# A transformer layer over 1,024 sequences on one Trainium2 core: the turn of x, a store and a load change their places in the step

## The reference

```python
q, k, v = ((x @ w + b) split into 8 heads of 16 features)
attn = softmax(q @ k^T / 4)                # per head, 128 x 128
out  = concat(attn @ v) @ wo + bo
n    = layernorm(x + out, ln1_g, ln1_b)
ff   = relu(n @ w1 + b1) @ w2 + b2         # 128 -> 512 -> 128
y    = layernorm(n + ff, ln2_g, ln2_b)
```

## Time and profile before

| | |
|---|---|
| median of 3 runs | 4271.92 us (4266.54 to 4272.6) |
| the profiled execution's own time | 4273.66 us |
| its span in the trace | 4271.9 us |
| granted TensorE clock, mean | 0.997 |
| busy: PE, PEld | 4104.8 us (96%), 3538.0 us (83%) |
| busy: DVE, ACT, POOL | 3669.8 us (86%), 3434.5 us (80%), 3723.4 us (87%) |
| DMA engines, mean busy share | some 0.8 in nearly every slice |

### The profile page before, as it was taken

The page is one execution under the profiler, slowest core; times in us unless marked ns, Lnnn a source line. Parts: engine busy times, 40 slices in busy tenths (PEclk is TensorE's granted clock), DMA queues, the critical chain, the costliest instruction groups (busy, mean ns, idle before and its releaser), DMA issues.

```text
span 4271.9 us, 150528 instructions
## 1 busy us (share of the span) xinstructions
PE 4104.8 (96%) x49930; PEld 3538.0 (83%) x49930; DVE 3669.8 (86%) x9740; ACT 3434.5 (80%) x5890; POOL 3723.4 (87%) x3864
## 2 busy tenths in 40 slices
PE   5999999999999999999999999999999999999997
PEld 4888888888888888888888888888888888888886
DVE  5888888888888888888888888888888888888885
ACT  4888888888888888888878888888888888888886
POOL 4888888888888888988888888888888888888987
PEclk9999999999999999999999999999999999999999
DMA  7788887888888888888778888887878888888883
GB/s 147 178 177 185 175 185 175 186 179 183 180 180 183 178 182 174 184 176 183 177 178 180 183 176 183 176 185 176 187 177 184 180 179 180 180 180 179 186 178 84
DMA packets 1970442, 755.81 MB, mean 177 GB/s; under 512 B 1181312, under 2 KB 1969536, under 8 KB 1969664
## 3 DMA queue, kind: packets, MB, share of 16 engines
q1 hardware_dynamic: 1662480, 605.71, 66.8%
q10 hardware_dynamic: 307184, 140.40, 12.3%
HBM read 202.51 MB, written 134.22 MB: 79 GB/s over the span
## 4 chain that ended last, share of the span: by engine, by line
PE 42%; issue 20%; ACT 10%; DVE 9%; SPq 5%; ACTq 5%; POOL 5%; DMA 3%; DVEq 1%; POOLq 0%
PE bankB L693 10%; PE bankC L693 9%; PE oT_ps L734 6%; SPq L252 5%; PE s_ps L707 5%; PE sT_ps L721 4%; ACT h_sb L397 4%; DMA stack<-parts 3%; PE bankC L670 3%; DVE xT_sb L502 2%; ACT parts L385 2%; PE bankA L670 2%; ACTq L430 2%; ACT parts L379 2%; PE bankB L670 2%
## 5 line engine op out<-in xcount | busy, mean ns | idle before, releaser
L417 ACT ACTIVATE prob_sb<-sT_ps 128x1024 f32<-128x1024 f32 x1024 | 1050.6, 1026 | 415.8 <-PE sT_ps L721 342.4
L547 DVE TENSOR_REDUCE max_sb<-s_ps 128x8 f32<-128x1024 f32 x1024 | 1220.2, 1192 | 6.9 <-PE s_ps L707 5.9
L278 POOL TENSOR_TENSOR parts<-rest_sb,parts 128x512 bf16<-128x512 f32 x512 | 584.4, 1162 | 243.0 <-ACT parts L385 243.0
L707 PEld LDWEIGHTS s_ps<-stack 96*128 96x128 bf16 x8192 | 463.9, 98 | 296.1 <-issue 181.4
L707 PE MATMUL s_ps<-stack 96*128 96x128 bf16 x8192 | 639.5, 221 | 42.0 <-DMA stack<-parts 24.0
L448 ACT ACTIVATE n_sb<-z_sb,shift,rs 128x128 f32<-128x128 f32 x1024 | 422.2, 483 | 276.1 <-POOL shift L323 276.0
L721 PE MATMUL sT_ps<-stack 99*128 99x128 bf16 x8192 | 627.9, 219 | 2.9 <-ACT prob_sb L417 2.9
L693 PE MATMUL bankB<-w_sb,h_sb 128*128 128x128 f32 x4096 | 525.2, 281 | 77.2 <-ACT h_sb L397 75.8
L693 PEld LDWEIGHTS bankB<-w_sb,h_sb 128*128 128x128 f32 x4096 | 476.5, 191 | 120.5 <-ACT h_sb L397 118.7
L734 PE MATMUL oT_ps<-prob_sb,v_ones 128*32 128x128 f32 x16384 | 554.0, 276 | 4.6 <-ACT prob_sb L417 3.3
L734 PEld LDWEIGHTS oT_ps<-prob_sb,v_ones 128*32 128x32 f32 x16384 | 416.4, 109 | 127.9 <-issue 89.4
(11 more groups left out here) (75 smaller groups left out, 8469.8 us busy)
## 6 DMA issues: line engine op xcount, KB each, us to landing
stack<-parts SPq DMA_DIRECT2D x3072, 128.0 KB, 3.6
x_blocks<-in_x SPq DMA_DIRECT2D x1024, 64.0 KB, 2.4
n_mem<-n_sb SPq DMA_DIRECT2D x256, 256.0 KB, 3.2
n_blocks<-n_mem SPq DMA_DIRECT2D x1024, 64.0 KB, 2.2
out<-out_sb ACTq DMA_DIRECT2D x256, 256.0 KB, 3.3
x_sb<-in_x ACTq DMA_DIRECT2D x255, 256.0 KB, 4.4
stack<-max_parts ACTq DMA_DIRECT2D x768, 8.0 KB, 2.2
h_sb<-in_L_conv_w SPq DMA_DIRECT2D x1, 256.0 KB, 3.1
```

The costliest lines, as they stand in the source:

```text
L278: pool.tensor_tensor(parts[:, r % 2, 3 * c + LO], rest_sb[:, c], parts[:, r % 2, 3 * c + MID], ALU.subtract).then_inc(lo_split, 1)
L417: act.activation(prob_sb[:, s % 2], sT_ps[:], ACT.Exp, scale=float(D) ** -0.5).then_inc(exp_done, 1)
L547: dve.reduce_max(max_sb[:, (r - lag) % 2, :, s], s_ps[:].rearrange("p (h k) -> p h k", h=H), AX.X).then_inc(max_done, 1)
L707: ins = pe.matmul(s_ps[:, h * P:(h + 1) * P], stack[0:PROD, (r - lag) % 4, 0, h, tok], stack[0:PROD, (r - lag) % 4, 1, h, tok], start=True ...
```

## The change

On VectorE, `turn_x` moves from behind the maxima of slot 0 to the head of the step, ahead of `turn_out(0)`. On ScalarE, the cast of `xT_sb` moves ahead of slot 0's exponential, and the issue of x's load moves from there to between `n_sb`'s and `m_sb`'s four applications. The output's store leaves ScalarE: SP issues it one step later (lag 9 instead of 8), between the store of n and the loads of x in blocks, and SP's loop therefore runs to lag 9. No instruction is added or dropped in the steady step and no tile changes its size.

```diff
--- before.py
+++ after.py
@@ -236,6 +236,9 @@
                 if live(t, r, 5):
                     sp.wait_ge(n_done, upto(t, r, 5, plus=1))
                     sp.dma_start(n_mem[(r - 5) % 2].rearrange("(s k) m -> k s m", s=SEQS), n_sb[:]).then_inc(n_stored, DMA)
+                if live(t, r, 9):
+                    sp.wait_ge(out_ready, upto(t, r, 9, plus=1))
+                    sp.dma_start(out_g[t + (r - 9)], out_sb[:, (r - 9) % 2]).then_inc(out_stored[(r - 9) % 2], DMA)
                 if live(t, r, -1):
                     if (v := upto(t, r, 0)) is not None:
                         sp.wait_ge(x_turned, v)
@@ -252,7 +255,7 @@
                             sp.dma_start(stack[j:PROD:len(Q_PARTS), r % 4, c].rearrange("d h x -> d (h x)"),
                                          parts[:, r % 2, 3 * c + part]).then_inc(stack_loaded[r % 2], DMA)
 
-            iterate(sp, step, 0, LEAD, LAST, 5)
+            iterate(sp, step, 0, LEAD, LAST, 9)
             sp.wait_ge(out_stored[(G - 2) % 2], upto_dma(0, G - 2, 0))
             sp.wait_ge(out_stored[(G - 1) % 2], upto_dma(0, G - 1, 0))
 
@@ -418,16 +421,12 @@
 
             def step(t, r):
 
-                exponentials(t, r, 0)
                 if live(t, r, 0):
                     act.wait_ge(x_turned, upto(t, r, 0, plus=1))
                     if (v := upto(t, r, 0)) is not None:
                         act.wait_ge(k_done, v)
                     act.activation(xT_parts[:, HI], xT_sb[:], ACT.Copy).then_inc(xT_hi, 1)
-                if live(t, r, 0) and (r > 0 or not isinstance(t, int)):
-                    if (v := upto(t, r, 1)) is not None:
-                        act.wait_ge(xb_done, v)
-                    act.dma_start(x_sb[:, r % 2], x_g[t + r]).then_inc(x_loaded[r % 2], DMA)
+                exponentials(t, r, 0)
                 if live(t, r, 7):
                     relu(t, r, 7, 2)
                     relu(t, r, 7, 3)
@@ -448,6 +447,10 @@
                         ins = act.activation(n_sb[:, s], z_sb[:, s], ACT.Identity, bias=shift[:, 0, s:s + 1],
                                              scale=rs[:, 0, s:s + 1])
                     ins.then_inc(n_done, 1)
+                if live(t, r, 0) and (r > 0 or not isinstance(t, int)):
+                    if (v := upto(t, r, 1)) is not None:
+                        act.wait_ge(xb_done, v)
+                    act.dma_start(x_sb[:, r % 2], x_g[t + r]).then_inc(x_loaded[r % 2], DMA)
                 if live(t, r, 8):
                     apply2(t, r, 8)
 
@@ -477,9 +480,6 @@
                                    ACT.Copy).then_inc(v_copied, 1)
                 if live(t, r, 2):
                     max_row(t, r, LO)
-                if live(t, r, 8):
-                    act.wait_ge(out_ready, upto(t, r, 8, plus=1))
-                    act.dma_start(out_g[t + (r - 8)], out_sb[:, (r - 8) % 2]).then_inc(out_stored[(r - 8) % 2], DMA)
 
             act.wait_ge(qk_loaded, N_QK * DMA)
             act.wait_ge(v_ones_set, 1)
@@ -575,11 +575,11 @@
 
             def step(t, r):
 
+                if live(t, r, 0) and (r > 0 or not isinstance(t, int)):
+                    turn_x(t, r)
                 if live(t, r, 4):
                     turn_out(t, r, 0)
                 row_max(t, r, 0)
-                if live(t, r, 0) and (r > 0 or not isinstance(t, int)):
-                    turn_x(t, r)
                 if live(t, r, 5):
                     dve.wait_ge(wo_done, upto(t, r, 5, plus=1))
                     dve.wait_ge(xb_done, upto(t, r, 5, plus=1))
```

## The result

The changed kernel takes 4247.61 us in the median of 10 runs (4237.61 to 4260.47), the one before 4268.78 us (4263.9 to 4277.23): a ratio of 0.9947 with a 95% interval of 0.9935 to 0.9959. It is faster, by some 21 us, where 84 were forecast. The time lies inside the stated range of 4152 to 4262 us, but only because the range was stretched to the first rival; of the forecast gain a quarter came.

A forecast was written before the change was run, and what follows sets the result against it. TensorE's stall before down, ending the chain turn, cast, relus, was taken as the bound, beside a ring with 0.28 us slack. 4273.66 - 72 (turn) - 12 (stack) = 4189.7 profiled, so 4188 us; 8-in-10 range 4152 to 4262.

The forecast's parts named there:

- the first rival: The stack takes over: its copies land no earlier, half of the 72 us lost, no 12 won; 4236 us, chance 17%.
- What bounds the kernel: TensorE's stall before down, 75.8 to 118.7 us, ends the chain turned x, cast, relu, relu; a ring is equally long.
- The turn and the ring: Earlier turn and cast give TensorE 0.25 to 0.39 us a step; the z-to-z ring's slack limits it to 0.28: 72 us.
- x's load between n and m: Its issue in ScalarE's stream hides under n's applications: nothing taken; bounds nothing and 0.40 + 0.14 us a step.
- The stack's landing: Copies slot 3's scores read land 1.2 us early; 12 us won, bounds 24 us won and the whole 72 lost.
- the signs that the prediction names: Profile checks: L693's wait under 30 us; stack wait beyond 40 means first rival; L693's wait gone, step above 16: wrong.
- The store on SP: ScalarE loses a 0.53 us issue, worth within the 0.39 a step; SP has room, so nothing is late.
- x in blocks: SP's loads for VectorE's turn land at 18.3 to 20.1, wanted at 20.53: in time, nothing charged.
- fourth rival: VectorE's head waits for x in blocks behind the store's writes: +133 us, 4405 us, chance 5%.
- x's issue exposed on the ring: Third rival: x's issue on ScalarE delays m and the exponential; 4338 us, or 4494 if it takes 1.01; chance 6%.
- nothing moves: Second rival: the ring has no usable slack, the exponential being late only by a latency; 4272 us, chance 6%.
- the forecast's own range: 4155 to 4215 us: 0.39 a step and all 24 us on one side, 0.22 a step on the other; forecast 62%.

The follow-up runs named there:

- e1: Changed kernel with x's load issued right behind the cast and the store back on ScalarE: 4269.09 us, ratio 1.0010 to the kernel before.
- e3: Changed kernel with x's load issued right behind the cast of x, the store staying on SP: 4168.14 us, ratio 0.9776 to the kernel before.
- e5: Kernel before with only the output's store moved to SP: 4239.27 us, ratio 0.9922 to the kernel before.
- e10: Changed kernel, x's load still between n and m, with SP issuing the store behind the stack's copies: 4240.77 us, ratio 0.9931 to the kernel before.
- e8: Changed kernel with x's load behind the cast and SP's store behind the loads of x in blocks: 4177.63 us, ratio 0.9776 to the kernel before.
- e9: Changed kernel with x's load behind the cast and SP's store behind the stack's copies: 4173.66 us, ratio 0.9776 to the kernel before.
- e2: Changed kernel with the store back at the end of ScalarE's step, x's load between n and m: 4230.69 us, ratio 0.9927 to the kernel before.
- e4: Changed kernel with x's load issued behind the split of q and k, the store on SP: 4256.91 us, ratio 0.9981 to the kernel before.
- e11: Changed kernel with x's load issued behind the two relus, the store on SP: 4170.87 us, ratio 0.9773 to the kernel before.
- e7: Changed kernel with x's load in its place but of one sequence of four, residual wrong for three: 4161.39 us, ratio 0.9740 to the kernel before.

## Why the prediction was wrong

**What bounds the kernel** was read rightly. Down's stall was the end of turn, cast, relu, relu, and it went away (118.7 to 5.3 us). The turn and the cast alone were not enough: in e1, which has only them, 69.5 us of it are left.

**The turn and the ring** were sized about rightly. The forecast gives 72 us to the turn, limited by the ring's slack of 0.28. From m's first application to the split of q and k, the part of the ring with that slack, the median of all steps is 2.76 us before and 2.45 in e3, 0.31 less. The time shows it where nothing hides it: e5 and e3 have the store on SP and x's load behind the cast, and differ by the turn and the cast alone; 0.9922 against 0.9776 is 1.46%, 62 us. By itself the same move brings nothing (e1). e3 beats the kernel before by 2.2%, 96 us, near the 84 forecast, but partly by luck: the turn is worth less than forecast there and the store (33 us) more.

**x's load between n and m** is the step that failed. Its issue was costed at nothing, and that was right: 1.56 us from n to m before and after. Its bytes were named ("travel beside the last copies of the stack, not beside the early ones") and given no price. They have one: a quarter of them in the same place brings 0.9947 down to 0.9740, 2.1% or 88 us; the whole load in an earlier place brings it to 0.9776, 1.7% or 73 us.

**The stack's landing** is the term in which this stands. It was booked as 12 us won. TensorE's wait grew from 24.0 to 87.7 us. Against e3, which has everything but the late load, it is 74 us more, and the time is 73 us more: 96 won less 73 lost are the 21 measured, within 2 us. Two readings led there. The slack before slot 3 was worked out as 1.2 us with the median landing of all twelve copies, 3.6 us, but the last three of a step of before took 3.8 to 4.0, and the row with 33 late steps said already that the spread reaches the reader. And the transfer that left the stretch helped the early copies (2.4 us, against a median of 3.6 before), for which nobody waits; from the first copy's issue to the last landing the whole takes 11.8 us, where it took 11.7. The first rival had the mechanism, at half its size and a chance of 17%; what it lacked was the cause, the transfer moved next to the last copy. Of the signs that the prediction names, two came against it: the wait for the stack is beyond 40 us, and L693's wait is gone while the step is still 16.25 us in the mean (16.35 before, 15.93 in e3; steps 14 to 249).

**The store on SP** was right by itself: e5 gives 0.78%, 33 us, more than the 12 booked, and the wait for the stack falls by the 12 or so that were booked (24.0 to 11.2). But the forecast said that nothing on SP is late, and that failed: the first copy of the stack was late in some 60 steps. SP's cover was thinner: four block loads took 2.56 us to issue in the step shown instead of 1.99 (medians of all steps 2.8 and 2.1), and in e10 n's store lands too late. Beside x's late load the store's worth stays open: e8, e9 and e10 move it within SP's queue and change nothing that the intervals tell, and e2's interval (0.9914 to 0.9939) just touches that of the changed kernel.

**x in blocks** landed in time, as forecast (1.0 us of waiting in all); e4 shows how near it was. The prediction says of its fourth rival that no row of before has a store ahead of x's blocks. One does: n's store stands ahead of them in the same queue, and they land in 2.4 us.

**x's issue exposed on the ring**, the third rival, is refuted by the 1.56 us; *nothing moves* by e3.

One bound was added up wrongly: 0.39 a step and 24 us are 124 us, so the forecast's own range starts at 4148, not at 4155, and so reaches below the range for 8 in 10. Nothing else hangs on it.

The version to take is e3 or e11: the change with x's load left near the cast. It beats the kernel before by 2.2%.

## What to carry to other kernels

A DMA issue has two prices, the time in its stream and the bytes beside other transfers. Here the second was paid by TensorE, which waits for the last copy of a group. Before a load is moved, ask which copy in flight at the new place completes a wait with little slack, and read that copy's landing in its own stretch, not the median of its line. When a step gets shorter, a wait that was late in a few steps can be late in many: 33 became 129 here, and 12 in e3, where the landing came sooner as well.

## What the runs showed of the hardware

- A read of 256 KB on ScalarE's queue, issued beside SP's last copies of 128 KB, took their landing from 2.4 us to 3.8 to 4.5 in the step shown; issued 6 us earlier it left them at 2.4 to 2.5 in a step of e3. In the median of all steps the last copy takes 3.8 us in the changed kernel, 3.1 in e3, 2.7 with a quarter of the bytes (e7) and 2.5 with the load issued after the last copy (e4).
- The issue of x's load never took over 0.51 us on ScalarE in the changed kernel and the kernel before, beside SP's copies as it is. In e3, where it is issued 1.5 us after the stack's first copy, its median is 0.41 us as well, but single issues take up to 1.31. The output's store, on the same stream and of the same shape, took up to 1.86 us in the kernel before.
- The store was worth 33 us when it went from ScalarE, beside the copies, to SP, ahead of x in blocks (e5). Its place in SP's queue made no difference with x's load early (e3, e8, e9). No run changes the issuing engine and keeps the time of the transfer, so whether the engine matters is not shown.
